# Spreading four probability-times-value jobs over the slot of an attention kernel, instead of running them in two pairs

## The reference, cut to what matters

```python
scores = jnp.einsum('bhqd,bhkd->bhqk', q, k) / math.sqrt(HD)
scores = scores + mask[None]
attn = jax.nn.softmax(scores, axis=-1)
out = jnp.einsum('bhqk,bhkd->bhqd', attn, v)
...
x = x + mha(xn, mask, in_proj_w[i], ...)
xn = layer_norm(x, ln2_w[i], ln2_b[i])
h = jax.nn.gelu(xn @ ffn1_w[i].T + ffn1_b[i], approximate=False)
x = x + (h @ ffn2_w[i].T + ffn2_b[i])
```

## Time and profile before

| | |
|---|---|
| runs | 1765.33, 1766.71, 1770.55 us |
| median of the runs | 1766.71 us |
| the profiled execution | 1765.33 us, its span 1763.5 us (1.8 us lie around it) |
| busy in the span | PE 1527.8, PE weight loads 1146.0, VectorE 1117.1, ScalarE 930.1, POOL 516.8 us |
| encoder slots | 64, 21.3 to 22.0 us each in the middle layers, 22.1 to 22.7 us in the last |
| expert slots | 16, near 15 us each |

### The profile page before, as it was taken

The page is one execution under the profiler, slowest core; times in us unless marked ns, Lnnn a source line. Parts: engine busy times, 40 slices in busy tenths (PEclk is TensorE's granted clock), DMA queues, the critical chain, the costliest instruction groups (busy, mean ns, idle before and its releaser), DMA issues. The chain is left out here.

```text
span 1763.5 us, 40986 instructions
## 1 busy us (share of the span) xinstructions
PE 1527.8 (87%) x12834; PEld 1146.0 (65%) x13024; DVE 1117.1 (63%) x3106; ACT 930.1 (53%) x1652; POOL 516.8 (29%) x908
## 2 busy tenths in 40 slices
PE   0777775699999989999999899999998999999996
PEld 0554443567777767777777677777776777677774
DVE  6677774456666656666666566666665666666663
ACT  3233332256566546566665565665655555555554
POOL 5222231122222222222222222222222234344433
PEclk9799998799999999999999999999999999999998
DMA  4343341222222222222222122222222222222220
GB/s 116 99 106 106 107 106 44 73 90 80 76 75 74 74 63 72 89 72 75 79 76 75 62 74 87 79 78 75 74 72 66 76 83 75 78 78 78 78 61 13
DMA packets 109892, 137.22 MB, mean 78 GB/s; under 512 B 14272, under 2 KB 95808, under 8 KB 109824
## 3 DMA queue, kind: packets, MB, share of 16 engines
q1 hardware_dynamic: 102176, 115.81, 23.1%
q0 software_dynamic: 7680, 20.98, 3.4%
HBM read 70.54 MB, written 65.01 MB: 77 GB/s over the span
## 5 line engine op out<-in xcount | busy, mean ns | idle before, releaser
L761 ACT ACTIVATE probs<-exp_ps 128x512 f32<-128x512 f32 x896 | 516.8, 597 | 648.4 <-PE exp_ps L872 507.6
L628 DVE TENSOR_REDUCE negm<-mxp 128x2 f32<-128x512 f32 (+1 forms) x1152 | 606.1, 566 | 252.8 <-PE mxp L847 238.1
L841 PE MATMUL mxp<-kst_l,qbd_l 127*128 127x256 f32 x2048 | 462.4, 333 | 67.9 <-DMA qbd_l<-split_L 64.4
L841 PEld LDWEIGHTS mxp<-kst_l,qbd_l 127*128 127x128 f32 x2048 | 332.8, 198 | 82.8 <-DMA qbd_l<-split_L 69.4
L867 PE MATMUL exp_ps<-qbd_l,kst_l 128*128 128x512 f32 x768 | 361.7, 491 | 5.3 <-DMA qbd_l<-negt 4.6
L454 POOL TENSOR_SCALAR veps<-mv 128x2 f32<-128x2 f32 x144 | 31.6, 219 | 931.5 <-DVE mv L586 928.3
L847 PE MATMUL mxp<-maskb,identb 128*128 128x256 bf16 x1024 | 293.5, 287 | 0.0
L896 PE MATMUL pvp<-probs,vst_l 128*32 128x256 f32 (+1 forms) x4096 | 193.0, 329 | 0.0
L674 DVE COPY ost<-pvp 128x512 f32<-128x512 f32 x80 | 55.3, 692 | 186.0 <-PE pvp L896 186.0
L872 PE MATMUL exp_ps<-masktb,identb 128*128 128x256 bf16 (+1 forms) x578 | 171.8, 297 | 0.0
L867 PEld LDWEIGHTS exp_ps<-qbd_l,kst_l 128*128 128x128 f32 x768 | 151.5, 197 | 21.2 <-issue 12.5
(11 more groups left out here) (93 smaller groups left out, 1923.6 us busy)
## 6 DMA issues: line engine op xcount, KB each, us to landing
split_L<-hi SPq DMA_DIRECT2D x256, 128.0 KB, 2.1
kst_l<-split_L SPq DMA_DIRECT2D x64, 384.0 KB
qbd_l<-split_L SPq DMA_DIRECT2D x256, 96.0 KB
split_L<-lo POOLq DMA_DIRECT2D x128, 128.0 KB, 2.1
split_F<-hi SPq DMA_DIRECT2D x64, 128.0 KB, 2.1
kst_f<-split_F SPq DMA_DIRECT2D x16, 384.0 KB, 3.8
qbd_f<-split_F SPq DMA_DIRECT2D x32, 192.0 KB, 4.4
split_F<-lo POOLq DMA_DIRECT2D x32, 128.0 KB, 2.4
```

Source lines behind the costliest of these rows:

```text
L628: dve.tensor_reduce(negm[:, s, qt, h0:h0 + 2], mxp[:, (plan.max_chunks * g + ch) % 3, :].rearrange("p (h t) -> p h t", h=2)[:, :, 0:keys], ...
L761: act.activation(probs[:, g[0], ch, :], exp_ps[:, (plan.exp_chunks * g[0] + ch) % 2, :], ACT.Exp, scale=plan.scale).then_inc(q.b_exp, 1)
L841: last = pe.matmul(mxp[:, bank, k * T:(k + 1) * T], qbd[plan.name][0:MAX_ROW, s, h, qt * P:(qt + 1) * P], kst[plan.name][0:MAX_ROW, s, g[0 ...
```

## The change

The list of the slot is edited so that each `pv` job stands alone: `pv` 0 moves from position k = 8 to k = 5, ahead of `qk+`; `pv` 1 stays at k = 8; `pv` 2 moves from behind `f1` to behind `negt` at k = 11; `pv` 3 stays last. The same list serves both branches; in the expert branch there is no `f1`, so `pv` 2 and 3 stay next to each other there. Nothing is computed differently, and no instruction is added or taken away.

```diff
             at("op+", s - 1) + at("qk", s + 2),
-            at("qk+", s + 2),
+            [("pv", s, 0)] + at("qk+", s + 2),
             at("end", s - 2) if last_layer else [],
             at("xn2", s - 1) if ff else [],
-            [("pv", s, 0), ("pv", s, 1)] + (at("xt2", s - 1) if ff else []),
+            [("pv", s, 1)] + (at("xt2", s - 1) if ff else []),
             at("xt2+", s - 1) if ff else [],
             at("end+", s - 2) if last_layer else [],
-            at("negt negt+", s + 1)]
+            at("negt negt+", s + 1) + [("pv", s, 2)]]
...
         out += at("f1 f1+", s - 1) if ff else []
-        out += [("pv", s, 2), ("pv", s, 3)] + at("pv+", s) + at("stack+", s + 2)
+        out += [("pv", s, GROUPS - 1)] + at("pv+", s) + at("stack+", s + 2)
```

## The result

The changed kernel took 1791.2 us in the median of four runs (1785.4 to 1795.2), the one before 1767.0 us (1765.3 to 1770.6): a ratio of 1.0136, 95% interval 1.0108 to 1.0164. The profiled execution took 1786.9 us, span 1785.0, against 1763.5 before: +21.5 us. The direction was forecast, the size was not: 1776.5 us was predicted, and the range ended at 1788.

What follows compares the result with a forecast made beforehand. TensorE was taken to bound the kernel, with stretch B almost continuous. Terms 10.6 - 1.8 + 0 + 1 + 0 = +9.8 us gave 1775.1 on the profiled execution, 1776.5 us against the median; range 1765 to 1788.

Steps and rivals of the forecast that it cites:

- step 6: Expert branch, 16 slots, only `pv` 0 moves: cost 0 if VectorE's train stays gapless, at most +5 us.
- slower by more: Rival, chance 0.11: `pv` 2 not hidden, half of 20 us, plus the expert bound, giving 1791 us.
- Step 1: `pv` 0 moved to k = 5: one more passage in and out, net +0.33 us a slot in B.
- Step 2: Encoder outside the last layer: the stall of piece 11 goes; with `pv` 0's cost +0.22 us in 48 slots, +10.6 us.
- the stall of piece 11: In B, piece 11 of `max` waits for VectorE's reduction 8, losing 0.11 us a slot.
- B: Stretch of a slot from the first `max` to `negt`, about 13.5 us; PE all but continuous, so added work moves the slot.
- Step 3: Last layer, 12 slots: reductions and piece 13 move by 0.50 us, 0.65 go out; -0.15 a slot, -1.8 us.
- VectorE's lag: Last layer: reduction 8 starts some 0.48 us late behind the mask of piece 8.
- Step 4: `pv` 2 ahead of `f1` in A: at most +0.33 us, within 0.72 us of idle time, so cost 0.
- A: Stretch from `negt` to the next slot's first `max`, about 7.9 us, set by the DMA chain stacking queries.
- Step 5: `pv` 3 stands 0.3 us later; in three slots at a layer's start `op`'s new weights get later: +1 us.
- faster: Rival, chance 0.09: lone jobs' passages cost nothing more and VectorE's lag goes, giving 1754 us.

Runs made afterwards that it cites:

- e2: New list for the expert branch only, old one for the encoder, against the kernel before: ratio 1.0059, +10.4 us.
- e1: New list for the encoder only, old one for the expert branch, against the kernel before: ratio 1.0072, 1776.6 against 1764.5 us.
- e4: Encoder only, just `pv` 2 moved from behind `f1` to behind `negt`, against the kernel before: ratio 1.0018, +3.2 us.
- e6: Encoder only, all four `pv` jobs in one train behind `f1`, against the kernel before: ratio 0.9809, -34 us.
- e7: Encoder only, `pv` 0 alone at k = 8 and `pv` 1, 2, 3 behind `f1`, against the kernel before: ratio 0.9807, -34 us.
- e5: Expert branch only, pairs in the old places but both jobs in the same columns, against the kernel before: ratio 1.0128, +22.6 us.
- e9: Encoder only, pair `pv` 0 and 1 moved whole from k = 8 to k = 6, against the kernel before: ratio 1.0055, +9.8 us.
- e10: All four encoder `pv` jobs behind `f1`, with `xt2` and its copy one position later, against the kernel before: ratio 0.9896.

## Why the prediction was off

The step that failed is step 6, the expert branch: "An expert job has half the matmuls and costs less than the 0.98 us above, and the pair at k = 8 gives its share back before piece 5 is due." The first half took the encoder's price as an upper end, but a job alone costs 0.99 us even before its passage in. The second half is the real fault: the pair went from 1.02 us to a job of 0.99 us, so it gave back 0.03 us. I had carried over the encoder's ratio of a pair to a single (1.44 to 0.79) without reading the expert pair's own rows and the column positions in the code: 16 matmuls in 1.02 us, while the encoder's 32 take 1.44, was a hint that was in the trace, since half of the encoder's 32 are only half as wide. So 0.99 us more and the passage lie ahead of piece 2, and VectorE's train, which "sets the pace there", got pauses of 0.22 us before piece 2 and 0.47 us before piece 5, the very pieces that step 6 names. My own condition ("as long as no gap opens in that train") was the right one; its bound of +0.33 a slot, +5 us in all, was the wrong one. Measured: +0.51 us a slot at full clock, +7.7 us in the profiled pair and +10.4 us in e2, where the sum had 0 and its bound 5.

That the time, 1791.2 us, is the number of the rival "slower by more", 1791, is luck. Of the 15 us that it adds, 10 were for `pv` 2 not being hidden, which the traces do not show, and 5 for the expert branch at its bound, which measured 8 to 10.

The encoder's steps, one by one:

- Step 1, a passage in of 0.17 us above the usual 0.04 and 0.79 us for a job alone: 0.21 and 0.79 us in the trace after. Confirmed.
- Step 2, the stall of piece 11 goes, net +0.22 us in B: +0.19 us, with no new stall. Confirmed, though the working has a wrong figure: a piece costs PE 0.36 to 0.37 us and not 0.54. The 1.09 us for a position of one `exp` and two pieces is right (1.08 to 1.11 in the rows), and it is what VectorE's two reductions of 0.49 us each have to fit in. The sum, +10.6 us, comes to 0.19 x 48 = 9.1.
- Step 3, the last layer -0.15 us a slot: -0.09. Piece 13 waits 0.26 us behind the mask of piece 12 (1625.17 to 1625.43) instead of 0.53. From the mask of piece 8 to piece 13 it is now 2.54 us (1622.89 to 1625.43), and it was 2.95: 0.41 us less, where VectorE's lag of 0.48 was to give 0.48.

```profile
1622.89 0.28 PE L847 MATMUL mxp<-maskb,identb 128*128 128x256 bf16 x1
...
1625.17 0.28 PE L847 MATMUL mxp<-maskb,identb 128*128 128x256 bf16 x1
1625.43 0.50 PE L841 MATMUL mxp<-kst_l,qbd_l 127*128 127x256 f32 x2
```

- Step 4, `pv` 2 hidden in A: A 7.48 before, 7.53 and 7.56 in the two traces after, 7.45 and 7.48 in e1 and e4. Confirmed by the traces; the timed runs of e4 leave room for up to 0.34%. How much cover there was is better read from the starts than from the idle time. In e6, A is 7.93 us in nearly every slot, all of it TensorE's own work, and e6 has two jobs of 0.65 us more in it than the kernel before; so this work is 6.63 us before (e7, with one such job more, has 7.27 as its shortest A, which fits) and, with 0.33 us more, 6.96 with `pv` 2 moved. The shortest A of the middle layers is 7.02 us in the change and 7.09 in e4, so the job was hidden in every slot. The 0.72 us of the earlier trace rows came near the mean cover of 0.85 us by two errors that go against each other: the mask missing from the records ahead of the first `max` makes the idle time too long, and the length of that mask, where it is recorded, too short. The 10.6 us for which PE waits for the stacked queries from 404 to 1430 us of the changed kernel must therefore be set against the 21.9 of e2, not against 33.3:

```profile
PE mxp L841 <- DMA qbd_l<-split_L: 10.6, 23, 0.8
```

- Step 5, three slots at the start of a layer: not told apart.

The encoder's sum of +9.8 us measured 12.7 us in e1 by timed runs (5.0 to 9.5 thousandths, 9 to 17 us) and 8.7 us between profiled executions, so it stands within what the runs can tell. What lies behind the last expert copy is 6.3 us longer than before in e1's trace, and 13.8 and 17.5 us in the two traces of the whole change; B of the middle layers is 10.3, 11.0 and 11.9 us of it. The "faster" rival falls: passages cost what the rows said. The page TensorEngine Tiling of the Trainium skill gave both halves of this case, in its section Key Properties. Its drain at a change of mode is what step 1 prices, and the trace agrees with 0.17 us. Its other rule, that tiles operate independently and can run in parallel, I weighed only between a job and its full-width neighbour, where the rows speak against it; it applied between two jobs with different columns, and e5 agrees with 1.02 against 1.85 us.

What stays open: the 3 us of e4, if they are real, and why the encoder's part is 7 to 11 us longer in the traces of the whole change than in e1's, when B of the middle layers makes up 2 us of this at most. That the changed kernel's runs scatter by 10 us and the first four of the kernel before by 5 needs no cause: 20 runs of the kernel before, beside e1, lie between 1758.6 and 1770.4 us, and the expert slots at the lower clock may account for most of the difference between the two traces of the changed kernel. Why the clock falls in some expert slots and not in others no run shows.

## What to carry to other kernels

Before a group of small matmuls is split, read the price of one and of two from the trace for each form of the group, together with the columns that each uses: jobs in different columns are nearly free beside each other, and splitting them pays the full price twice. In a kernel with an order written by hand, split the slot at the point where a DMA chain ends, and ask of each stretch what sets its length; here work belonged in the stretch that waits for the chain, and moving two jobs there, with the one transpose and copy that this uncovered, took 3.4% off where spreading them cost 1.4%. A pause on one engine can be another engine's cover. With one job left at k = 8 (the change, e7) no wait appeared; with both gone (e9, e6) `xt2` waited for VectorE's normalisation, and with `xt2` and its copy moved later as well (e10) `f1` waited for ScalarE's copy.

## What was not expected of the hardware

- Eight matmuls with 32-column weights at two column positions take 0.99 us from their start to the next full-width start; eight more at the other two positions add 0.03 us; eight more at the same two add 0.86 us.
- Moving a train of 32 such matmuls from k = 8 to k = 6 (e9) cost 9.8 us with no instruction and no passage added, by the wait it uncovered.
- In the expert branch stretch B of a slot with 3 to 4 us at the lower clock was 0.5 to 0.9 us longer with the pair (8.5 to 8.9 us against 7.98), and 1.3 to 1.8 us longer with the jobs apart (9.81 to 10.27 against 8.49).
